# The W1 column sums: the eight d tiles added on VectorE before the matmuls

## The reference, cut to what matters

```
h   = rmsnorm(layernorm(x)) * gamma
q, kv, a = split(h @ w_qkva.T);  a = sigmoid(a)
y_t = a_t * y_{t-1} + kv_t                       # scan over the tokens
x   = x + q * y
n   = layernorm(x)
gate = softmax(n @ Wg + bg)                      # 8 experts
h1_e = relu(n @ W1_e + b1_e)                     # W1_e: 1024 x 128
out = x + sum_e gate_e * (h1_e @ W2_e + b2_e)
```

## Time and profile before

| | |
|---|---|
| median of 3 runs | 343.1 us (342.95 to 343.72) |
| the profiled execution | 343.28 us |
| its span, slowest core (core 3) | 341.7 us (all cores: 340.3 to 341.7) |
| PE busy | 326.7 us, 96% |
| DVE busy | 186.0 us, 54% |
| ACT busy | 102.9 us, 30% |
| POOL busy | 46.3 us, 14% |
| chain that ended last | PE 90% of the span |

### The profile page before, as it was taken

The page is one execution under the profiler, slowest core; times in us unless marked ns, Lnnn a source line. Parts: engine busy times, 40 slices in busy tenths (PEclk is TensorE's granted clock), DMA queues, the critical chain, the costliest instruction groups (busy, mean ns, idle before and its releaser), DMA issues.

```text
span 341.7 us, 4873 instructions; the slowest of 8 cores (340.3 to 341.7 us)
## 1 busy us (share of the span) xinstructions
PE 326.7 (96%) x1601; PEld 150.8 (44%) x1601; DVE 186.0 (54%) x425; ACT 102.9 (30%) x158; POOL 46.3 (14%) x61
## 2 busy tenths in 40 slices
PE   7689999399999999999999999999999999999995
PEld 2335444254444444444444444444444444444442
DVE  0835467513678469545578368453778346533332
ACT  2462326873225310501425410504225520200000
POOL 3750000101121210000221210001121210000000
PEclk9999999879999999999999999999999999999999
DMA  7999999999920300099850300298100300254033
GB/s 157 218 156 174 230 234 191 217 210 172 217 79 1 126 1 0 2 245 249 150 218 1 126 0 1 63 206 287 63 1 0 126 0 0 65 130 178 0 123 123
DMA packets 18840, 40.47 MB, mean 118 GB/s; under 512 B 10040, under 2 KB 10328, under 8 KB 17792
## 3 DMA queue, kind: packets, MB, share of 16 engines
q1 hardware_dynamic: 15616, 25.47, 26.6%
q0 software_dynamic: 3200, 14.70, 22.7%
HBM read 40.15 MB, written 8.42 MB: 142 GB/s over the span
## 4 chain that ended last, share of the span: by engine, by line
PE 90%; DVE 3%; DMA 2%; ACT 2%; issue 1%; DVEq 0%; SPq 0%; ACTq 0%
PE ps L578 48%; PE ps L637 16%; PE ps L661 16%; DMA xtok<-xt 2%; PE ps L658 2%; PE ps L641 2%; DVE bst L261 2%; PE ps L373 2%; ACT xn L277 1%; PE ps L549 1%; PE ps L606 1%; PE ps L289 1%; PE ps L399 1%; PE ps L387 1%; ACT L430 0%
## 5 line engine op out<-in xcount | busy, mean ns | idle before, releaser
L578 PE MATMUL ps<-pb,wq 128*128 128x512 bf16 x768 | 172.4, 382 | 0.6 <-DVE pb L481 0.6
L578 PEld LDWEIGHTS ps<-pb,wq 128*128 128x128 bf16 x768 | 74.9, 98 | 89.1 <-issue 5.4
L637 PE MATMUL ps<-pb,w 128*128 128x512 bf16 x256 | 60.5, 379 | 0.0
L661 PE MATMUL ps<-h1g,w 128*128 128x512 bf16 x256 | 60.5, 379 | 0.0
L614 POOL TENSOR_TENSOR xb<-xb,sc 128x512 f32<-128x512 f32 x24 | 30.4, 1266 | 178.0 <-DVE sc L600 138.4
L591 DVE TENSOR_TENSOR_SCAN sc<-asig,carry,ps 128x512 f32<-128x512 f32 x24 | 30.7, 1280 | 38.8 <-ACT sqr L361 22.9
L585 ACT ACTIVATE asig<-ps 128x512 f32<-128x512 f32 x32 | 19.1, 597 | 103.5 <-PE ps L578 90.9
L664 DVE TENSOR_TENSOR xb<-ps,xb 128x512 f32<-128x512 f32 x32 | 22.1, 691 | 33.4 <-PE ps L661 33.4
L661 PEld LDWEIGHTS ps<-h1g,w 128*128 128x128 bf16 x256 | 25.1, 98 | 30.1
L637 PEld LDWEIGHTS ps<-pb,w 128*128 128x128 bf16 x256 | 24.9, 98 | 30.2 <-issue 0.4
L643 DVE SCALAR_TENSOR_TENSOR h1g<-ps,grep 128x512 bf16<-128x512 f32 x32 | 21.9, 686 | 17.6 <-PE ps L641 17.3
(11 more groups left out here) (100 smaller groups left out, 173.8 us busy)
## 6 DMA issues: line engine op xcount, KB each, us to landing
xtok<-xt SPq DMA_DIRECT2D x12, 512.0 KB, 10.8
outd<-xb SPq DMA_DIRECT2D x12, 512.0 KB, 5.4
wq<-wqd POOLq DMA_DIRECT2D x7, 768.0 KB, 23.3
grep<-gscr SPq DMA_DIRECT2D x4, 1024.0 KB, 6.0
xb<-xd SPq DMA_DIRECT2D x8, 512.0 KB, 6.7
w<-xt POOLq DMA_DIRECT2D x4, 512.0 KB, 29.0
xb<-xd POOLq DMA_DIRECT2D x4, 512.0 KB, 47.1
w<-w1d POOLq DMA_DIRECT2D x2, 1024.0 KB, 52.1
```

The source lines that it names most:

```text
L578: mm[i] = PE.do(lambda e, k=k: e.matmul(ps[banks[i]][:], wq[:, j, i, k, :], hbc[:, k, :], start=(k == 0), stop=(k == KC - 1)), h[k] if j = ...
L637: PE.do(lambda e, k=k: e.matmul(ps[b][:], w1[:, e_, k, :], xbf_of[c][:, k, :], start=(k == 0), stop=False), C[c]["xbf"][k] if e_ == 0 else ...
L661: t = PE.do(lambda e, e_=e_: e.matmul(ps[b][:], w2[:, d, e_, :], h1g[:, e_, :], start=False, stop=(e_ == E - 1)), C[c]["h1g"][e_], w2_t[d ...
```

## The change

For each expert, `w1_presum(e_)` puts three operations on DVE. The first reduces W1's tile 128 x 8 x 128 (bf16) over the eight d tiles to 128 sums in f32; the view is turned so that the d tile is the innermost axis, at a step of 128 elements. The second makes the bf16 high part, the third subtracts it to give the bf16 low part. The parts lie in `xn`. `w1_sums(h)` then needs two matmuls (high and low) in place of eight, and waits for the last presum of its half. The presums stand at hooks (2, 1), (3, 1), (4, 1), (5, 1), (6, 1), (6, 2), (7, 0) and (7, 1); at (6, 2) the presum stands ahead of `w1_sums(0)`.

```diff
+        ws_f = xn[:, 0:2, :].rearrange("p a b -> p (a b)").bitcast(F32)
+        ws_b = xn[:, 2:4, :].rearrange("p a b -> p (a b)")
+        ws_tok = [None] * E
+
+        def w1_presum(e_):
+            sl = slice(e_ * H, (e_ + 1) * H)
+            t = DVE.do(lambda e: e.tensor_reduce(ws_f[:, sl], w1[:, e_].rearrange("p k h -> p h k"), AX.X, ALU.add),
+                       w1_t[e_ // 4], *xn_free)
+            t = DVE.do(lambda e: e.tensor_copy(ws_b[:, sl], ws_f[:, sl]), t)
+            ws_tok[e_] = DVE.do(lambda e: e.tensor_tensor(ws_b[:, E * H + e_ * H:E * H + (e_ + 1) * H], ws_f[:, sl],
+                                                          ws_b[:, sl], ALU.subtract), t)
+
         def w1_sums(h):
             b = ring_take()
-            for k in range(KC):
-                t = PE.do(lambda e, k=k: e.matmul(ps[b][:], selw[:], w1[:, 4 * h:4 * h + 4, k, :], start=(k == 0),
-                                                  stop=(k == KC - 1)),
-                          w1_t[h], ms["selw"], ring_free[b] if k == 0 else None, tick=(k == KC - 1))
+            for k in range(2):
+                t = PE.do(lambda e, k=k: e.matmul(ps[b][:], selw[:], ws_b[:, k * E * H + h * 512:k * E * H + (h + 1) * 512],
+                                                  start=(k == 0), stop=(k == 1)),
+                          ws_tok[4 * h + 3], ms["selw"], ring_free[b] if k == 0 else None, tick=(k == 1))
+            for i in range(NT):
+                xn_free[i] = t
...
+        for e_, p in enumerate([(2, 1), (3, 1), (4, 1), (5, 1), (6, 1), (6, 2), (7, 0), (7, 1)]):
+            add(hk, p, lambda e_=e_: w1_presum(e_))
         add(hk, (6, 2), lambda: w1_sums(0))
         add(hk, (7, 2), lambda: w1_sums(1))
```

## The result

The changed kernel takes 358.54 us, median of 5 runs (358.0 to 360.18), against 343.1 before: a ratio of 1.046, 95% interval 1.043 to 1.049. The forecast was 351.5 with a range to 357.0. Its sign and its two stalls are there, its size isn't. Some executions, of the kernel before too (3 of its 23 beside the experiments), take 8% longer or more, with a lower granted clock on some cores, and the ratios leave them out.

What follows compares the result with a forecast made beforehand. PE was taken to bound the kernel, with DVE near full in this stretch. Stalls of 2.73 and 6.11 less the 2.59 gain, about 6.2, plus 2.1 for the clock, on 343.28 gave 351.6, about 351.5 for the median; range 348.3 to 357.

Steps and rivals of the forecast that it cites:

- the first stall: PE waits at rows_step(1, 3) behind the late Exp, then for the gates; PE 2.73 us late.
- the second, larger one: PE waits 6.11 us for the last presum before the second w1_sums.
- the cast: Second operation of a presum on DVE, making the bf16 high part: 0.24 us.
- the subtraction: Third operation of a presum on DVE, making the bf16 low part: 0.29 us.
- the 12 matmuls: W1 sums on PE go from 16 matmuls to 4: 2.59 us less on the chain, the whole gain.
- the W1 loads: Loads take 52.1 us, issued at 19.3 and 20.3; first presum at 93.4, so its wait costs nothing.
- The replay of DVE's list: Presums of 1.86 us followed through DVE's timeline: gates 4.16 us late, last W1 sum 6.24 us late.
- the reduce's term: One presum's reduce of 1024 elements on DVE takes 1.21 us, from a PSUM reduce at 1.0 ns an element.
- slow reduce: Rival: the reduce takes up to 2.4 us, up to 9.6 us more in all, 361 us; chance 0.13.
- the clock: TensorE's granted clock falls in the stall at the last W1 sums, costing 1.4 to 2.8 us, taken as 2.1.
- early fall: Rival: clock falls already in the first stall, group 6's scan up to 1.7 us later, 353.3 us; chance 0.08.
- Hidden: Rival: presums fit in DVE's idle time, only the 2.59 us gain is left, 340.7 us; chance 0.04.

Runs made afterwards that it cites:

- experiment 7: Changed kernel with three presums on DVE and five on POOL, moved to hooks where these have room, away from the gate work: 341.02 us, ratio 0.9928 to the kernel before.
- Experiment 1: Changed kernel with the reduce adding eight neighbouring elements of W1 (step 1, not 128), counts and places unchanged: 354.32 us, ratio 1.0305 to the kernel before.
- experiment 2: Changed kernel with the eight reduces' summands at steps of 1, 2, 4 up to 128 elements, for durations alone: 356.69 us in one execution.
- experiment 8: Changed kernel with the reduces adding 2, 3, 4, 5, 6, 7, 8 and 8 tiles at step 128, for durations: 379.2 to 379.6 us in three executions.
- experiment 9: Changed kernel with all presums behind the gate work and useless matmuls (29 and 36) filling PE's two stalls: 357.2 us, ratio 1.0394 to the kernel before.
- experiment 4: Changed kernel with presums issued but nobody waiting for them, w1_sums keeping its eight matmuls: 357.02 us, ratio 1.0392 to the kernel before.
- experiment 5: Changed kernel with useless matmuls keeping PE busy in both stalls (14 and 38), presums at the same hooks: 356.37 us, ratio 1.0371 to the kernel before.
- experiment 6: Changed kernel with all eight presums moved behind the gate work, nothing filling PE's stalls: 384.24 us, ratio 1.1212 to the kernel before.
- experiment 3: Changed kernel with the reduce adding only two of the eight d tiles, everything else the same: 348.07 us, ratio 1.0125 to the kernel before.

## Why the prediction was wrong

**Right.** That DVE's free half isn't where the work goes; that the first stall is at rows_step(1, 3) through the Exp and the second, larger one at the last W1 sums; the cast 0.24 (0.23), the subtraction 0.29 (0.29), all of a presum but its reduce (2.54 us less 1.90 is 0.64, forecast 0.65); the 12 matmuls at 2.6 us, as experiment 7 returned them; the W1 loads in time. The replay of DVE's list was sound: with 2.55 us a presum, its steps have the gates 6.2 us late (core 5: 113.77 against 108.04 before, and its scan of group 2 is 0.40 earlier, so 6.13) and the last sum 11.8.

**The step that failed: the reduce's term, "I take 1.21".** It took 1.90, and the replay counts the difference of 0.69 us eight times, 5.5 us. The nearest row was a reduce of PSUM at 1.0 ns an element, and I gave it more weight than the scan's 2.2 on the other side; the case stood in the text as the rival "slow reduce", at 0.13. The Trainium skill's rule in "SBUF — State Buffer", the paragraph on SBUF cachelines, cited beside it, pointed the right way. Experiment 1, which makes the term true, moves the kernel to 353.6: 4.9 of the 7.0 us between 351.5 and 358.5. The eight summands lie 256 bytes apart, and experiments 1, 2 and 8 show that their distance and their number are the cost.

**The second step: the clock, at one place only.** I counted a fall behind the second stall (1.4 to 2.8; core 5 lost 3.0) and gave a fall in the first a chance of 0.08. It fell there in the change (3.22 us idle) and even in experiment 1, where PE sat idle for 1.83 us. Its price was forecast rightly, up to 1.7 us through the scan of group 6: 1.22 us in the change, on three of eight cores, and some 1.2 of the 1.55 in experiment 1. With the cast's 0.46, a wait that the sum didn't have, that is the other 2 us.

The sum in core 5's trace: 11.8 from the list, 1.22 for the late scan, 0.46 for the cast and 3.0 for the clock are 16.5. Measured are 357.0 - 341.1 = 15.9 between the spans of that core, and the 0.4 by which it began this stretch earlier: 16.3.

**The rivals.** "Slow reduce" and "early fall" both came true at once; each was priced, their joint case wasn't. At 1.90 us the slow reduce alone gives 343.1 + 11.8 + 2.1 = 357.0, just the range's end; the rest took the time past it. "Hidden" was false here, but the mechanism is real once the presums stand where the room is: experiment 7.

## What to carry to other kernels

Before work goes to an engine that the page shows half idle, read that engine's timeline in the very stretch, and replay its list; when the new work exceeds the idle time there, neither another order (experiment 9) nor taking away the wait (experiment 4) helps, only less work or another stretch. A stall of PE can be paid twice, since the clock can fall in it: keeping PE busy gave back 3 of 15 us (experiment 5). Of an operation that no row shows, take the access pattern into the price: a reduce over a far axis isn't the reduce of the nearest row, and if two rivals can come true together, the range has to hold them together.

## What the runs showed of the hardware

- A DVE reduce of bf16 over the innermost axis of the view: 1.0 ns an element with summands up to 8 bytes apart, 1.7 to 1.8 from 16 bytes on, at eight summands. With two or three summands 256 bytes apart it is 1.0 again (0.42 and 0.55 us for 256 and 384 elements), with four 1.7 (1.02 us for 512).
- TensorE's granted clock fell to 0.5 where PE had been idle for 1.83 us and had begun again (experiment 1, within 109 to 110 us), with no idleness like the 4.3 us ahead of the fall in the earlier trace rows. It did so on all eight cores.
- Two stalls of 6.86 and 6.51 us with restarts were followed by some 160 us at 0.81 on four to eight cores in each of four executions (experiment 6), and weren't in four of five when PE was kept busy in them (experiment 9). What brings the level on isn't shown: two cores of experiment 8 had it too, the change with its longer stall didn't.
- The cast of the fifth presum waited 0.46 us longer for its reduce in the change and in experiments 1 to 5 and 8 alike (0.46 to 0.47), at the same place in the list, and not with the presums in other places (experiments 6, 7 and 9). What it waits for isn't shown.
- A DVE cast of 128x128 that takes 0.23 us alone took 0.65 to 1.12 us where a POOL add ran at the same time (experiments 7 and 3).
